# State space chunks one slot deeper in a fused two-layer kernel's pipeline, with silu for some gates

## The reference

```python
# state space half: one sequence, d_inner 256, 4 heads of 64, state 128, convolution over 4 tokens
n = rmsnorm(xn) * norm_w;  proj = n @ in_proj_w.T       # z, x_ssm, B, C, dt_raw
x_conv = silu(conv_b + sum_k pad(x_ssm)[k:k+L] * conv_w[:, k])
dt  = softplus(dt_raw + dt_bias);  dA = exp(-exp(A_log) * dt)
h_t = h_{t-1} * dA_t + (dt_t * xh_t) outer B_t;  y_t = h_t C_t      # scan over tokens
attn = xn + ((y + D * xh) * silu(z)) @ out_proj_w.T
# feed-forward half, all products times a scale per output
h = silu(lin(xn, w1)) * lin(xn, w2)                     # 128 -> 512
h = gelu(lin(h, h1));  h = gelu(lin(h, h2))             # 512 -> 512
out = x + attn + lin(h, w3)                             # 512 -> 128
```

## Time and profile before

| | us |
|---|---|
| median of 3 runs | 629.19 |
| the runs | 625.9, 629.19, 635.57 |
| the profiled execution | 634.12 |
| its span, first to last instruction | 632.4 |
| busy: TensorE, ScalarE, VectorE, GpSimd | 567.3, 462.6, 406.8, 147.7 |
| mean granted TensorE clock | 0.978 of 2.4 GHz |

### The profile page before, as it was taken

The page is one execution under the profiler, slowest core; times in us unless marked ns, Lnnn a source line. Parts: engine busy times, 40 slices in busy tenths (PEclk is TensorE's granted clock), DMA queues, the critical chain, the costliest instruction groups (busy, mean ns, idle before and its releaser), DMA issues.

```text
span 632.4 us, 11258 instructions
## 1 busy us (share of the span) xinstructions
PE 567.3 (90%) x3972; PEld 330.8 (52%) x3977; DVE 406.8 (64%) x1038; ACT 462.6 (73%) x629; POOL 147.7 (23%) x175
## 2 busy tenths in 40 slices
PE   4569999999999999999897799787898998998998
PEld 3234334444343433333334477365576887887887
DVE  6985865556444343475415655678878898898753
ACT  2368987999989999888576265579585676676663
POOL 2044222020110021103600745104022322323231
PEclk9879999999999999999989999899998999999999
DMA  7112002013422220210317121200000000000000
GB/s 220 30 41 68 2 1 68 1 41 108 165 101 101 86 85 1 86 50 13 105 24 224 59 81 39 80 0 2 0 2 1 1 18 1 1 18 1 1 18 18
DMA packets 31175, 31.00 MB, mean 49 GB/s; under 512 B 6912, under 2 KB 21024, under 8 KB 31120
## 3 DMA queue, kind: packets, MB, share of 16 engines
q1 hardware_dynamic: 29872, 27.71, 14.1%
q0 software_dynamic: 1248, 2.57, 1.1%
HBM read 13.44 MB, written 12.89 MB: 42 GB/s over the span
## 4 chain that ended last, share of the span: by engine, by line
PE 56%; DVE 25%; ACT 6%; issue 6%; POOL 2%; DMA 2%; SPq 2%; another core or an unknown queue 1%; DVEq 0%; ACTq 0%; POOLq 0%
PE ps L1361 17%; PE ps L1342 8%; PE ps L92 3%; PE ps L94 3%; PE ps L93 3%; DVE r L2408 2%; PE ps L1662 2%; DVE xn L2408 2%; PE ps L1425 2%; PE ps L1438 2%; DVE r L2507 2%; PE ps L1259 1%; ACT r L972 1%; PE ps L1536 1%; SPq L715 1%
## 5 line engine op out<-in xcount | busy, mean ns | idle before, releaser
L972 ACT ACTIVATE r<-ps 128x1024 f32<-128x1024 f32 x272 | 258.3, 1035 | 35.1 <-PE ps L1342 28.8
L1361 PE MATMUL ps<-r 128*32 128x512 f32 (+3 forms) x1280 | 148.2, 550 | 2.2 <-DVE r L2075 0.9
L844 POOL TENSOR_SCALAR_AFFINE_SELECT r<-r 128x512 f32<-128x512 f32 (+1 forms) x80 | 47.3, 594 | 219.9 <-ACT r L972 219.7
L1342 PE MATMUL ps<-r2r 32*128 32x512 f32 (+3 forms) x640 | 79.0, 453 | 8.9 <-DMA r2r<-r2r 4.3
L1342 PEld LDWEIGHTS ps<-r2r 32*128 32x128 f32 x640 | 34.7, 185 | 51.5 <-ACT r L972 21.5
L887 POOL TENSOR_TENSOR r<-r 128x512 f32<-128x512 f32 x16 | 23.3, 1458 | 135.9 <-ACT r L1178 135.9
L1361 PEld LDWEIGHTS ps<-r 128*32 128x32 f32 x1280 | 27.8, 109 | 42.7 <-issue 30.1
L94 PE MATMUL ps<-r2r 128*128 128x512 f32 (+1 forms) x104 | 39.0, 375 | 0.0
L93 PE MATMUL ps<-r2r 128*128 128x512 f32 (+1 forms) x88 | 32.9, 374 | 0.0
L822 POOL DMA_INDIRECT rows_by_expert<-r x16 | 17.7, 1107 | 64.1 <-DVE r L1999 60.2
L1156 ACT ACTIVATE r1r<-r 128x512 fp32r<-128x512 f32 x16 | 10.1, 631 | 28.0 <-DVE r L2436 27.9
(11 more groups left out here) (403 smaller groups left out, 1224.2 us busy)
## 6 DMA issues: line engine op xcount, KB each, us to landing
rows_by_expert<-r SPq DMA_DIRECT2D x34, 258.0 KB, 2.4
r2r<-r2r SPq DMA_DIRECT2D x60, 64.0 KB, 2.0
r<-in_f_W SPq DMA_DIRECT2D x1, 2048.0 KB, 9.4
r<-rows_by_expert SPq DMA_DIRECT2D x23, 64.5 KB, 1.8
res<-in_x SPq DMA_DIRECT2D x4, 256.0 KB, 4.8
r<-in_g_h1T SPq DMA_DIRECT2D x1, 1024.0 KB, 5.7
r<-in_g_h2T SPq DMA_DIRECT2D x1, 1024.0 KB, 7.9
r<-rows_by_token SPq DMA_DIRECT2D x4, 256.0 KB, 4.0
```

The source lines that it names most:

```text
L844: pool.affine_select(blk, blk, pattern, ALU.is_ge, nothing, base=0, channel_multiplier=-1).then_inc(s_msk, 1)
L972: act.activation(probs[:, n % PBUFS, :, :], ps[:, b:b + 2, :], ACT.Exp).then_inc(s_exp, 1)
L1342: m = pe.matmul(ps[:, 2 * (n % SBUFS) + h, at:at + TB - query], kst[32 * j:32 * j + 32, group, P * kt:P * kt + P], qst[32 * j:32 * j + 32, ...
L1361: m = pe.matmul(ps[32 * j:32 * j + 32, 6, query:TB], vp[:, kt, group, :], probs[:, (2 * v + j // 2) % PBUFS, j % 2, at:at + TB - query], s ...
```

## The change

Three things are done.

1. The z gates are one activation by Silu each, straight from PSUM (`z_gates` for `z_tanh` and `gated_z`), and so is block 0's convolution (`first_convolved` for `sums_tanh(0, m)` and `gated_c(0, m)`). Blocks 1 to 3 keep tanh, with taps and bias halved beforehand (`halves`), so that the result is the true value; the halvings of `owT`, `d2` and `dt` go.
2. `chunk(i+1)` moves from behind `state(i)` (slot 2i+1) to the even slot 2i, behind `projected(i-1)`. `chunk_started(i+1)` moves to VectorE's odd slot 2i+1, and `decays(i+1)` to ScalarE's odd slot, behind the gelu (and, in slots 5 and 7, behind `up_tanh`). A new semaphore `s_cb` tells that `chunk_started` has read its products. `state_carried` and `weighted` stay in the even slot.
3. `taps_added` moves to slots 1 and 3, the `gated_c` to slot 5, `last_tap` to slot 0 and `sums_tanh` to slot 4.

```diff
-            def z_tanh(b):
+            def z_gates(b):
                 for k in range(2):
                     act.wait_ge(s_pj, proj_done(f"z{k}", b))
-                    if b >= 1:
-                        act.wait_ge(s_z2, 2 * (b - 1) + k + 1)
-                    act.activation(th[:, k, :], ps[:, proj_bank(f"z{k}", b), :], ACT.Tanh, scale=0.5
-                                   ).then_inc(s_zth, 1)
+                    act.activation(z2[:, k, b * TB:b * TB + TB], ps[:, proj_bank(f"z{k}", b), :], ACT.Silu
+                                   ).then_inc(s_z2, 1)
...
+            def first_convolved(m):
+                act.wait_ge(s_cvt, m + 1)
+                act.wait_ge(s_halo, 2)
+                act.activation(xc[:, m, 0, HALO:], conv_sums(0, m), ACT.Silu).then_inc(s_xc, 1)
...
                     if o == 0:
                         gated_high(b, FO - 1)
-                    if o == 2 and b < NB - 1:
+                        if not b:
+                            decays(0)
+                    middle_gelu(b, o)
+                    if o == 0 and b < NB - 1:
                         for m in range(MI):
                             last_tap(b + 1, m)
-                    if o % 2 == 0:
-                        decays(SLOT(b, o) // 2)
-                    middle_gelu(b, o)
+                    if o % 2:
+                        decays(SLOT(b, o) // 2 + 1)
                 for o in range(FO):
                     if o and b < NB - 1:
                         gated_high(b + 1, o - 1)
-                    if o == 2 and b < NB - 1:
-                        for m in range(MI):
-                            sums_tanh(b + 1, m)
-                    if o % 2 == 0:
-                        decays(SLOT(b, FO + o) // 2)
                     last_gelu(b, o)
                     if b < NB - 1:
                         up_tanh(b + 1, o)
+                    if o == 0 and b < NB - 1:
+                        for m in range(MI):
+                            sums_tanh(b + 1, m)
+                    if o % 2 and SLOT(b, FO + o) // 2 + 1 < NCH:
+                        decays(SLOT(b, FO + o) // 2 + 1)
...
             def chunk(i):
                 if i:
-                    pe.wait_ge(s_cx, 2 * i)
+                    pe.wait_ge(s_cb, i)
                     pe.wait_ge(s_ce, 2 * i)
...
             def chunk_units(s):
                 if s % 2:
                     state(s // 2)
+                else:
+                    if s:
+                        projected(s // 2 - 1)
                     if s // 2 + 1 < NCH:
                         chunk(s // 2 + 1)
-                elif s:
-                    projected(s // 2 - 1)
...
-                step.mark(dve.tensor_scalar(owT, owT, 0.5, None, ALU.mult))
                 step.mark(dve.tensor_tensor(f3, f3, along(w3s_bc, FO), ALU.mult))
-                step.mark(dve.tensor_scalar(d2, d2, 0.5, None, ALU.mult))
+                dve.wait_ge(s_convw, 16)
+                step.mark(dve.tensor_scalar(halves, row[:, 284:294], 0.5, None, ALU.mult))
...
-            for m in range(MI):
-                gated_c(0, m)
             xn_low(0)
-            gated_z(1)
             xn_low(1)
-            gated_z(2)
-            gated_z(3)
...
-                    if s % 2:
+                    if s == 0:
+                        chunk_started(0)
+                        weighted(0)
+                    elif s % 2 == 0:
+                        state_carried(s // 2 - 1)
+                        weighted(s // 2)
+                        if o == 0:
+                            down_added(b - 1)
+                    else:
                         if s >= 3:
                             chunk_added(s // 2 - 1)
                         if o == 1 and b:
                             finished(b - 1)
-                    elif o == 0:
-                        chunk_started(s // 2)
-                        if b:
-                            state_carried(s // 2 - 1)
-                        weighted(s // 2)
-                        if b:
-                            down_added(b - 1)
-                    else:
-                        state_carried(s // 2 - 1)
-                        chunk_started(s // 2)
-                        weighted(s // 2)
-                        if b < NB - 1 and o < 6:
-                            taps_added(b + 1, (o // 2 - 1,))
-                        elif b < NB - 1:
+                        if s // 2 + 1 < NCH:
+                            chunk_started(s // 2 + 1)
+                        if b < NB - 1 and o in (1, 3):
+                            taps_added(b + 1, (o // 2,))
+                        elif b < NB - 1 and o == 5:
                             for m in range(MI):
                                 gated_c(b + 1, m)
```

More of the change, by code:

```diff
@@ L147, in build @@
         convb = row[:, 292:294]
+        halves = row[:, 324:334]
+        halfw, halfb = halves[:, 0:8].rearrange("p (m k) -> p m k", m=MI), halves[:, 8:10]
         d2 = row[:, 294:296]
@@ L315, in build @@
         ea = r3[:, k0 + 320:k0 + 324]
[L316 removed]
         c0 = k0 + 1536
         first_sums = r3[:, c0 + 1280:c0 + 2304].rearrange("p (m t) -> p m t", m=MI)
[L319 removed]
         conv_sums = lambda b, m: first_sums[:, m] if not b else (xn_flat[:, 0:TB], r2[:, 12292:12292 + TB])[m]
[L321 removed]
+        conv_tanh = lambda m: (r2[:, 0:TB], r2[:, 11780:11780 + TB])[m]
         xc_tokens = lambda m, i: xc[:, m, i // TPB, HALO + P * (i % TPB):HALO + P * (i % TPB) + P]
@@ L464, in build @@
         s_cx = sem("chunk_operands_from_dve")
+        s_cb = sem("chunk_products_read_by_dve")
         s_cy = sem("chunk_outputs")
@@ L1087, in last_tap @@
                     act.wait_ge(s_xc, 2 * (b - 1) + m + 1)
-                act.activation(conv_sums(b, m), xc[:, m, b, HALO:], ACT.Identity, bias=convb[:, m:m + 1],
-                               scale=convw[:, m, KW - 1:KW]).then_inc(s_cva, 1)
+                taps, bias_ = (halfw, halfb) if b else (convw, convb)
+                act.activation(conv_sums(b, m), xc[:, m, b, HALO:], ACT.Identity, bias=bias_[:, m:m + 1],
+                               scale=taps[:, m, KW - 1:KW]).then_inc(s_cva, 1)
+            def first_convolved(m):
+                act.wait_ge(s_cvt, m + 1)
+                act.wait_ge(s_halo, 2)
+                act.activation(xc[:, m, 0, HALO:], conv_sums(0, m), ACT.Silu).then_inc(s_xc, 1)
             def sums_tanh(b, m):
                 act.wait_ge(s_cvt, 2 * b + m + 1)
-                if b:
-                    act.wait_ge(s_pj, len(PROJ))
-                    act.wait_ge(s_xc, 2 * b)
-                act.activation(conv_tanh(b, m), conv_sums(b, m), ACT.Tanh, scale=0.5).then_inc(s_xth, 1)
+                act.wait_ge(s_pj, len(PROJ))
+                act.wait_ge(s_xc, 2 * b)
+                act.activation(conv_tanh(m), conv_sums(b, m), ACT.Tanh).then_inc(s_xth, 1)
             def xn_high(b):
@@ L1115, in _ @@
             roots_of(3)
-            z_tanh(0)
+            z_gates(0)
             tokens_read(2)
@@ L1128, in _ @@
             for m in range(MI):
-                sums_tanh(0, m)
+                first_convolved(m)
             xn_high(0)
-            z_tanh(1)
+            z_gates(1)
             taken(3)
@@ L1134, in _ @@
             xn_high(1)
-            z_tanh(2)
+            z_gates(2)
             centred(3)
-            z_tanh(3)
+            z_gates(3)
             act.wait_ge(s_dta, 1)
@@ L2388, in xs_low @@
                                   ).then_inc(s_pjv, 1)
-            def gated_z(b):
-                toks = slice(b * TB, b * TB + TB)
-                for k in range(2):
-                    dve.wait_ge(s_zth, 2 * b + k + 1)
-                    dve.scalar_tensor_tensor(z2[:, k, toks], th[:, k, :], 1.0, ps[:, proj_bank(f"z{k}", b), :],
-                                             ALU.add, ALU.mult).then_inc(s_z2, 1)
             def taps_added(b, ms=range(MI)):
@@ L2407, in taps_added @@
                         sums = conv_sums(b, m)
-                        added = dve.scalar_tensor_tensor(sums, xc[:, m, b, k:k + TB], convw[:, m, k:k + 1], sums,
+                        taps = halfw if b else convw
+                        added = dve.scalar_tensor_tensor(sums, xc[:, m, b, k:k + TB], taps[:, m, k:k + 1], sums,
                                                          ALU.mult, ALU.add)
@@ L2415, in gated_c @@
             def gated_c(b, m):
-                dve.wait_ge(s_xth, 2 * b + m + 1)
+                dve.wait_ge(s_xth, 2 * (b - 1) + m + 1)
                 if b < NB - 1:
                     dve.wait_ge(s_halo, b + 2)
-                dve.scalar_tensor_tensor(xc[:, m, b, HALO:], conv_tanh(b, m), 1.0, conv_sums(b, m), ALU.add, ALU.mult
+                dve.scalar_tensor_tensor(xc[:, m, b, HALO:], conv_tanh(m), 1.0, conv_sums(b, m), ALU.add, ALU.mult
                                          ).then_inc(s_xc, 1)
@@ L2448, in _ @@
             middle_weights_low(1)
-            gated_z(0)
             xs_low(3)
```

(2 more changed lines are left out.)

8 lines of the change are left out of this document (3 added, 5 removed).

## The result

| | before | after |
|---|---|---|
| median | 628.52 us (4 runs) | 644.20 us (4 runs) |
| the runs | 625.90 to 635.57 | 641.43 to 645.95 |
| the profiled execution, its span | 634.12, 632.4 | 644.50, 642.8 |
| busy: TensorE, ScalarE, VectorE, GpSimd | 567.3, 462.6, 406.8, 147.7 | 574.2, 464.8, 397.3, 146.4 |
| mean granted TensorE clock | 0.978 | 0.965 |

A forecast was written before the change was run, and what follows sets the result against it. TensorE was taken to bound the loop, ScalarE to set the pace before it. Terms: -10.1 + 1.3 + 11.6 + 3.1 + 3.0 = +8.9 us, taking the median from 629.2 to 638.1 us; range 630 to 643, wider 625 to 646.

The forecast's parts named there:

- waits and clock of before that go: In the loop, TensorE's waits for `up_gated` (5.7), for GpSimd's multiply (2.9) and 1.5 of clock vanish: -10.1 us.
- table load: Before the loop, silu adds one ScalarE table load ahead of L1139's Exp: +1.3 us, bounds 0 and 1.28.
- slot 2, three waits: In blocks 0 to 2, `projected` waits for `state_carried` behind the taps: 4.0 + 3.8 + 3.8 = 11.6 us, bounds 7.6 and 12.1.
- clock behind them: Behind the new slot-2 waits, two clock drops in three at 1.54 us each: +3.1 us, bounds 0 and 4.6.
- slot 6, three waits: `decays` ahead of the next split makes `projected` wait 0.65 to 1.75 us, three times: +3.0 us, bounds 2.0 and 5.3.
- last block: Block 3 has no taps, so no slot-2 wait; `projected(12)` may wait up to 0.5 us, in the high bound only.
- A: Rival: the loop's waits go and nothing takes their place, -8.8 us, 620 us; chance 0.13.
- B: Rival: waits only exchanged, taps free of GpSimd, clock at 2.4 GHz, silu free: -0.5 us, 628 to 631; chance 0.2.
- C: Rival: VectorE becomes the bound, its in-order waits for `gated_high` growing about 1 us at three places a block: 646 us; chance 0.17.
- The signs: L2433 and L892 waits vanish; three `projected` waits of 3 to 4 us, three short; clock 0.5; extra load; second block 49 us.
- One sign of being wrong: Wrong if loop waits sum under 8 us, a block lasts under 45.6, or the loop begins earlier than 457.

The follow-up runs named there:

- the first experiment: The changed kernel with the taps back in slots 2 and 4, behind `weighted`; 627.96 us in one run, before 628.67.
- the third rebuilt version: Kernel before with deeper chunks, slot 5's split before exponentials, taps in slots 2 and 4 (the latter behind `up_gated`), slot 5's `gated_c` behind `up_gated(b+1,1)`; 622.47 us, ratio 0.9912.
- the pipeline part alone: The changed kernel with tanh gates instead of silu, chunks a slot deeper and taps in slots 1 and 3 kept; 641.66 us against 628.61, ratio 1.0222.

## Why the prediction was right, and where it was short

The stretch behind the first layer grew by 15.4 us, where the sum said 8.9. By its terms, from the four blocks of after against the floors (42.93 us, and for block 0 41.04, the mean of 41.07 in the first experiment, 44.70 less 1.47 and 2.16, and 41.01 in the third rebuilt version). The clock's term is what is left of a block over floor and waits:

| term | forecast | measured |
|---|---|---|
| waits and clock of before that go | -10.1 | -10.4 |
| table load | +1.3 | +1.24 |
| slot 2, three waits | +11.6 | 4.37 + 3.67 + 3.67 = +11.7 |
| clock behind them | +3.1 | 2.28 + 2.80 + 2.76 = +7.8 |
| slot 6, three waits | +3.0 | 3 x 1.58 = +4.7 |
| last block | 0 | +0.3 |
| sum | +8.9 | +15.4 |

**The slot-2 waits** came where and nearly as long as the count from rows had them: 3.8 was forecast for block 1 and 3.67 came, 4.0 for block 0 and 4.37 came, so that the sum fits better than its parts, which is luck. VectorE's chunk start was put at 509.05 to 510.6, with the taps to 514.8, and it was 508.46 to 510.0 and 514.2, in a block that begins 0.54 us earlier (501.48 against 502.02). The first experiment shows that the taps' place is the cause, the one without GpSimd that 1.93 us of it in block 1 and 1.16 in block 0 (4.37 to 3.21) is contention.

**The clock** is the term that was mis-sized, by 4.7 us of the 6.5 missing. "I take two drops in three, 3.1": a drop was priced at 1.54 us, from the single one in the trace of before, behind a wait of 2.44 us. All three waits dropped it, and each was of the long kind, 2.3 to 2.8 us. The upper bound (4.6) used the same price three times, so it was no bound. What the trace of before could not show is that there are two lengths, and the pipeline part alone has a short one behind 4.39 us and both behind 3.67. Which comes goes with when the clock falls, not with how long the wait is: early in the three waits of after, 1.1 to 1.75 us before their end, late or behind the wait in every short case. No run shows what sets that moment, so the term stays at 1.7 or 2.8 us a wait. The clock missing behind the end of each wait of after, 2.5, 2.7 and 2.9 us, agrees with the term, and keeping TensorE busy through the wait gave 7.4 us back.

**The slot-6 waits** were right in place and order (the split ahead of the exponentials removes them) and within their bounds of 0.65 to 1.75; I took 1.0 where 1.58 was true, because the 1.1 us that `state_carried` loses beside GpSimd was put down as an upper bound only. In the timeline after, its first product (L2521) takes 1.51 us in that slot and 0.41 in slot 2. The shares were off the other way round as well: without GpSimd's multiplies 0.23 us is left, under the lower bound of 0.65.

**What goes** went in full, but "the taps leave slot 4 [...]: the 5.7 us go" gives only half a cause. Moved alone, the taps took little away: 4.3 of the 5.7 us stayed at `up_gated`, since the exponentials stood ahead of `up_tanh` and handed the delay on, and what went came back in the waits for L892 (5.3 us instead of 2.9) and in one of 1.85 us in slot 2. It needs the chunk start and its exponentials out of the even slot. With them out, the taps may stay in slot 4: the first experiment has no wait for `up_gated` either.

**Silu** cost one load. That the two profiles give 1.24 us for it, so near the 1.3, is luck: the same stretch varies by 2 us between the kernels with the same gates. The load of 1.28 us has the next activation 0.02 us behind it. The figure of the Trainium skill (ScalarE: Activation LUTs, What ACT_TABLE_LOAD costs), some 1380 ns of drain on top of the load, would make it 2.7 us. The timeline shows no such time, but the ratio of the kernel with silu alone allows for 0.9 to 3.4 us and so does not decide; it rests on the timeline.

**The rivals.** A (620) and B (628 to 631) were in reach of the same idea, not of this order of it: B asked for taps free of GpSimd and a clock that stays up, and the kernel without GpSimd's multiplies, which has both in its second block, took 629.5. C (646) comes near in time, yet not by its mechanism: VectorE was busy for 37.96 of 50.98 us and was no bound; late work is not much work.

**The signs.** All that were named came, with one wait of 4.37 us instead of 3 to 4 and a block of 50.98 instead of 49. One sign of being wrong came too, in its letter: the loop begins at 452.2, earlier than 457. It was badly chosen, since the first layer of this execution was 5.0 us shorter; counted from the table load behind that layer the loop begins 1.24 us later.

## What to carry to other kernels

When work is moved in an in-order queue, count from rows what stands behind it and who waits for that: the count from rows gave 11.6 us where 11.7 came. Work that nobody waits for belongs behind the last thing that is awaited in its slot, not in the slot that looks emptier. A wait in the bounding engine is priced with the clock behind it, and with a bound for it that is larger than the one drop that happens to be in the trace.

## What the runs showed of the hardware

- **The clock behind a wait.** In the loops of all the kernels together the granted clock fell to 0.50 (1.2 GHz) during or behind 14 of TensorE's waits: of 1.95, 2.06, 2.44 (in before and with silu alone), 3.21, 3.67 (six times) and 4.37 to 4.39 us (three times). It did not behind one of 2.16, one of 2.06, and any of 1.89 or less. The clock missing in windows of 1 us adds up to 1.70 or 1.71 us in nine of them and to 3.41 or 3.42 in the other five, nothing in between, and both kinds follow the same wait of 3.67 us. The wait's length does not tell them apart; the moment of the fall does, as the granted clock of short windows around it gives it. In the five of 3.41 the clock fell 0.9 to 1.75 us before the wait ended, in the nine of 1.70 it fell 0.2 us before that at the earliest and 1.3 us behind it at the latest. What sets the moment stays open.
- **VectorE beside GpSimd.** Three taps of 128x512 take 2.32 us alone and 4.25 us beside two GpSimd multiplies; a product of 128x256 takes 0.42 us alone, and 1.26 when it begins 0.29 us behind a multiply. When it begins 0.19 us ahead of the multiply it keeps its 0.42. The Trainium skill (SBUF — State Buffer, Who interferes with whom) describes the port pair that the two engines share as an exclusive lock: whichever instruction starts first has it to its end. These two pairs of rows agree: the stretched product ends at 527.98, 0.29 us behind the end of the multiply at 527.69. So does the one of 1.51 us in after, which ends at 540.52, 0.28 us behind GpSimd's at 540.24.
- **Order alone.** The same instructions with tanh gates and deeper chunks, in five orders, gave 641.7, 627.2, 623.8 (one run), 622.5 and 622.4 us (before beside them 628.0 to 630.1): 3% of the whole, with the same work on every engine.
